# Six buffers for gathered expert rows in place of four, and padding tails written by two queues

## What is computed

```python
q, k = relu(x @ Wq.T + bq), relu(x @ Wk.T + bk)          # 16 heads of 16
v = x @ Wv.T + bv
q_, k_ = concat(q*sin, q*cos), concat(k*sin, k*cos)      # by position
kv = einsum('nld,nlm->ndm', k_, v)
z = 1 / max(einsum('nld,nd->nl', q_, k_.sum(1)), 1e-4)
x = layernorm(x + (einsum('nld,ndm->nlm', q_, kv) * z) @ Wo.T + bo)
topv, topi = top_k(x @ router_w.T, 2);  w = softmax(topv)
out = sum over the 2 chosen experts e of  w_e * (gelu(x @ w1[e].T) @ w2[e].T)   # 256 -> 512 -> 256
x = layernorm(x + out)
```

## Time and profile before

| | |
|---|---|
| median of 3 runs | 925.64 us (923.71 to 933.85) |
| the profiled execution | 932.11 us |
| its span in the trace | 930.3 us |
| PE matmuls busy | 801.9 us, 86% |
| PE weight loads busy | 761.2 us, 82% |
| DVE busy | 622.1 us, 67% |
| ACT busy | 529.6 us, 57% |
| POOL busy | 454.9 us, 49% |
| DMA moved | 108.70 MB, 117 GB/s on average |
| granted TensorE clock, mean | 0.958 of full speed |

### The profile page before, as it was taken

One profiled execution on the slowest core, in us unless ns is written; L12 is line 12 of the kernel. 1 busy time (PEld: TensorE's weight loads), 2 busy tenths in 40 slices (PEclk: granted clock), 3 DMA queues, 4 the chain that ended last, 5 costly groups with the idle time before them and its releaser, 6 DMA issues.

```text
span 930.3 us, 21892 instructions
## 1 busy us (share of the span) xinstructions
PE 801.9 (86%) x7136; PEld 761.2 (82%) x7136; DVE 622.1 (67%) x1836; ACT 529.6 (57%) x1064; POOL 454.9 (49%) x517
## 2 busy tenths in 40 slices
PE   5999999999998688888889888878999978888880
PEld 5888988988998688878888888878999978888870
DVE  3335888888888587766777566645555667767763
ACT  4556676766766445555554454444655546656653
POOL 3651566666775265554654455432343334434442
PEclk9999999999999799999999999989999999989995
DMA  6461322332332222322222232522222535546544
GB/s 193 151 220 67 104 101 93 123 108 92 113 112 76 81 86 81 97 76 92 92 74 88 75 104 75 164 78 64 81 81 81 187 132 177 202 140 215 185 175 135
DMA packets 46821, 108.70 MB, mean 117 GB/s; under 512 B 8571, under 2 KB 18815, under 8 KB 44672
## 3 DMA queue, kind: packets, MB, share of 16 engines
q1 hardware_dynamic: 31184, 65.18, 22.8%
q0 software_dynamic: 12960, 33.84, 9.9%
q10 hardware_dynamic: 2576, 8.39, 2.3%
HBM read 64.91 MB, written 46.44 MB: 120 GB/s over the span
## 4 chain that ended last, share of the span: by engine, by line
DMA 14%; PE 14%; issue 14%; DVE 6%; POOL 4%; SPq 3%; ACT 1%; POOLq 0%; DVEq 0%; ACTq 0%
PE PS L726 9%; DMA token_rows<-xg 8%; DMA xg<-expert_rows 6%; PE PS L713 3%; POOL token_rows L1710 2%; PE PS L698 2%; DVE xg L1448 2%; SPq L436 2%; DVE hT L1439 1%; DVE xgT L1431 1%; SPq L437 1%; DMA z<-token_rows 1%; POOL zve L1716 1%; POOL expert_rows L1646 1%; DVE z L1465 1%
## 5 line engine op out<-in xcount | busy, mean ns | idle before, releaser
L1710 POOL DMA_INDIRECT token_rows<-xg x142 | 165.1, 1163 | 302.4 <-DVE xg L1448 276.3
L726 PE MATMUL PS<-w,hT 128*128 x1704 | 240.3, 300 | 6.9 <-issue 5.4
L726 PEld LDWEIGHTS PS<-w,hT 128*128 128x128 f32 x1704 | 226.8, 204 | 14.0 <-issue 13.3
L713 PE MATMUL PS<-xgT,w1s 128*128 128x256 f32 x1704 | 220.6, 286 | 1.8 <-DVE xgT L1431 1.8
L713 PEld LDWEIGHTS PS<-xgT,w1s 128*128 128x128 f32 x1704 | 212.6, 194 | 2.6 <-DVE xgT L1431 2.4
L971 ACT ACTIVATE hg<-PS 128x512 f32<-128x512 f32 x142 | 84.3, 595 | 154.0 <-PE PS L713 146.5
L1646 POOL DMA_INDIRECT expert_rows<-rows,idx x128 | 135.9, 1062 | 56.2 <-issue 44.1
L1431 DVE TENSOR_TENSOR xgT<-PS,xgT 128x512 fp32r<-128x512 f32 x71 | 49.0, 691 | 139.8 <-ACT xgT L965 116.4
L1423 DVE TENSOR_TENSOR w1s<-w,w1s 128x1024 fp32r<-128x1024 f32 x71 | 86.9, 1224 | 22.2 <-issue 16.1
L698 PE MATMUL PS<-cst,xg 128*128 128x128 f32 x284 | 47.3, 292 | 57.5 <-DMA xg<-expert_rows 57.4
L1439 DVE TENSOR_TENSOR hT<-hg,hT 128x512 fp32r<-128x512 f32 x142 | 91.2, 684 | 1.7 <-issue 1.7
(11 more groups left out here) (175 smaller groups left out, 1315.5 us busy)
## 6 DMA issues: line engine op xcount, KB each, us to landing
xg<-expert_rows SPq DMA_DIRECT2D x71, 260.0 KB
z<-token_rows SPq DMA_DIRECT2D x15, 1024.0 KB
xraw<-in_xT SPq DMA_DIRECT2D x32, 256.0 KB
xtok<-in_x SPq DMA_DIRECT2D x32, 256.0 KB
out_y<-z ACTq DMA_DIRECT2D x15, 512.0 KB, 3.3
w_raw<-in_w2T SPq DMA_DIRECT2D x8, 512.0 KB, 3.9
w<-in_w1T SPq DMA_DIRECT2D x8, 512.0 KB, 5.3
token_rows<-xg POOLq DMA_INDIRECT x142
```

The source lines that it names most:

```text
L713: mm = nc.tensor.matmul(PS[:, gH[part], f * TILE:(f + 1) * TILE], w1s[:, s % 2, b, k * F + c0:k * F + c0 + P], xgT[:, s % 2, a, k, :], sta ...
L726: return nc.tensor.matmul(PS[:, gY, h * D:(h + 1) * D], hT[:, s % 2, a, k, h * P:(h + 1) * P], w2[:, bass.ds(e, 1), b, k * D:(k + 1) * D] ...
L1710: nc.gpsimd.indirect_dma_start(yd, bass.IndirectOffsetOnAxis(ap=row[:, C_DST:C_GATE].bitcast(U32), axis=0), row[:, 0:D], None, bounds_chec ...
```

## The change

`NXG` goes from 4 to 6 and the slots get a new order. `gather` reads the row number first and waits for its slot after that. The waits on the first stage, which belong to places in memory, move from steps 2 and 3 to steps 3 and 4. The eight padding tails are shared: SP writes four of them at the place where it wrote eight, ACT's queue the other four, two in each of the half steps 60 and 61 (step 30). The amount of arithmetic is the same on each engine. The places of the token loads and of the `load`s on SP's queue are counted from NXG, so a load that stood behind the gather of step s + 4 stands behind that of s + 6.

```diff
-        NXG = 4
-        XG_SLOTS = (2, 3, 1, 0)
+        NXG = 6
+        XG_SLOTS = (0, 5, 4, 3, 1, 2)
...
+        def region_tail(eng, engine, e):
+
+            row = nc.values_load(tails_i[0:1, e:e + 1], engines=[engine], min_val=0, max_val=E * REGION - TILE)
+            eng.dma_start(ex[bass.ds(row, TILE), :].rearrange("(p h) c -> p (h c)", h=2),
+                          ex[E * REGION:, :].rearrange("(p h) c -> p (h c)", h=2)).then_inc(s_tail, 16)
...
             def gather(s):
+
                 row = nc.values_load(steps[1:2, s:s + 1], engines=[ENG.SP], min_val=0, max_val=E * REGION)
+                if s >= NXG:
+                    sp.wait_ge(s_y[s % NXG], s // NXG * 32)
                 sp.dma_start(xg[:, XG_SLOTS[s % NXG]], ex[bass.ds(row, TILE), :].rearrange("(p h) c -> p h c", h=2))\
                     .then_inc(s_xg[s % NXG], 16)
-
-            def freed(s):
-
-                sp.wait_ge(s_y[s % NXG], s // NXG * 32)
...
-                if s >= NXG:
-                    freed(s)
-                if s == 2:
+                if s == 3:
                     sp.wait_ge(s_tail, 16)
                     sp.wait_ge(state_step, STATE * (B - 1) + STATE_READ)
-                if s == 3:
+                if s == 4:
                     sp.wait_ge(state_step, STATE * B)
                 gather(s)
...
             sp.wait_ge(table_step, TAILS)
-            for e in range(E):
-                row = nc.values_load(tails_i[0:1, e:e + 1], engines=[ENG.SP], min_val=0, max_val=E * REGION - TILE)
-                sp.dma_start(ex[bass.ds(row, TILE), :].rearrange("(p h) c -> p (h c)", h=2),
-                             ex[E * REGION:, :].rearrange("(p h) c -> p (h c)", h=2)).then_inc(s_tail, 16)
+            for e in range(E // 2):
+                region_tail(sp, ENG.SP, e)
...
             for s in range(FULL_STEPS, STEPS):
-                freed(s)
                 gather(s)
...
+                elif 5 <= n < 7:
+                    act.wait_ge(table_step, TAILS)
+                    for e in range(E // 2 + 2 * (n - 5), E // 2 + 2 * (n - 5) + 2):
+                        region_tail(act, ENG.Activation, e)
```

## The result

The kernel before took 924.67 us (median of 4 runs beside the changed one), the changed kernel 844.01 us (841.35 to 846.08, 4 runs). The ratio is 0.916, with a 95% interval from 0.908 to 0.924: 8.4% faster. The forecast was 863 us with 850 as its low end, so the direction and the mechanism held, and the gain was forecast 19 us too small.

A forecast was written before the change was run, and what follows sets the result against it. The four-slot gather ring was taken to hold PE, with slots waiting for sends to land. Gains of 25 + 9.5 + 2 + 29 = 65.5 us from 932.1 gave 866.6; half the 6 us offset made 863 us, range 850 to 886.

The forecast's parts named there:

- Six slots, 600 to 657: Second stage around the padding tails, 7 steps: at the clean 6.69 us a step a gain of 10.3, taken as 9.5.
- 657 to 731: Second stage, 11 steps running alone: from 6.69 towards 6.47 us a step, at most 2.4 us, taken as 2.
- 731 to 892: Second stage, 20 steps beside the last layernorm: a gain of 29 us, ends 18 and 32.
- 331 to 600: Second stage, 29 steps beside attention pairs: 23.0 us waits plus 7.1 clock, less 5 returned as other waits; gain 25.
- The offset: Profiled execution before lay 0.7% above the runs' median; up to 6 us come off, half taken.
- Reading ahead: SP's gather, row number read ahead of the slot wait: hidden, 0; 0.7 us per binding turn if slack were gone.
- Tails: Padding tails on two queues: PE's 3.9 us wait at step 33 goes; price on ACT 0 to 5.3 us, taken 1.
- Rival 1: DVE sets the pace beside the last layernorm: gain there 17 to 18, about 880 us with returned waits; chance 0.14 (shared).
- Rivals 2 to 4: The second: landings stretch beside the last layernorm, ring stays tight, 882 to 890 us, chance 0.08; others listed below.
- rival 3: No change: the gather waits for SP's order of loads, not for its slot; about 925 us, chance 0.05.
- rival 4: Slower: SP's gathers run two further ahead and their reads collide with the sends; say 940 us, chance 0.03.
- Signs: Second stage: L698 wait under 5 us, clock 0.99 or more, L726 about 0.132 us each, steps beside layernorm 6.4 to 6.7.

## Why the prediction was right in kind and too small

**The bound.** Right. The turn of the four slots held PE. The gather's wait, 51.2 us in the four stretches, is gone with six slots, and most of it is back with six slots held as four.

**Six slots, 600 to 657.** I gave 9.5 and it was 13.75. The step that failed is "7 steps at the clean 6.69". The stretch 657 to 731 looked clean since L698 waits for only 0.9 us in it, but its ring was tight. Six of its steps began with rows that had only just landed. A pair of such steps (start 664.25 to 677.59) took 13.34 us, two of after take 12.38, and the row names a wait of 0.19. So each late landing cost some 0.9 us, of which 0.16 was listed on average (0.98 / 6, by the gaps ahead of the transposes).

**657 to 731.** I gave 2, at most 2.4, and it was 5.5. Here the floor failed: "towards 6.47", which was PE's busy time over eleven. PE's busy time held the slowed matmuls behind each late landing (transposes 0.66 in place of 0.60, L726 3.23 in place of 3.11). The same 573 instructions were busy for 71.18 us before and 68.05 after. The shortest step there was 6.29; that a step with its rows in time takes 6.19 is shown by the runs with five and six slots. The same row had a better floor: PEld was busy for 68.73 us, 6.25 a step.

**731 to 892.** I gave 29 with 32 as the upper end, and it was 35.3. It is the same floor: 20 steps at 6.47 are 129.4 us, and the stretch took 125.81. With 6.19 for 6.47 the upper end would have been 20 x (8.05 - 6.19) = 37.

**331 to 600.** I gave 25 and it was 30.8. What PE was idle (length less busy time) fell from 37.4 to 18.6 us. That is 18.7 back, where I had 23.0 of gather waits less 5 of others, so this term was right in its sum. The others did return: L585 went from 1.2 to 8.4 us, L681 from 1.2 to 3.7, L562 from 6.8 to 3.6. What PE was busy fell from 231.6 to 219.5 us, 12.1 back, and this is the term that failed: I had put 7.1, from the rows of L726 alone. They gave 98.90 - 90.89 = 8.0. The rest lies in other matmuls, 1.5 us in L562 and 1.0 in the transposes of L698, against 1.3 more in L713, with the slow one of step 31; what is left can't be given to a line, since the records of the lines overlap.

**PE's busy time as a whole.** By the same subtraction the four stretches gave back 18.7 + 8.4 + 2.4 + 22.8 = 52.4 us of idle time and 12.1 + 5.3 + 3.1 + 12.5 = 33.0 of busy time. Priced were 51.2 less 5 = 46.2 us of waits and 15.6 of slowed matmuls. The other price that the prediction gives, 24 us from the clock column, would have put the forecast at 855, still 11 too high. L726 gave 227.7 - 209.3 = 18.4.

**The offset.** I took half of the 6 us between the profiled execution and the median of before. The profiled execution of after lies 0.6 us above its median: nearly all of it vanished.

**Summed up:** 866.6 was worked out for the profiled execution and 844.6 came. The four stretches missed by 5.8 + 4.25 + 3.5 + 6.3 = 19.9 us, and 2.1 lie outside them. The last three of these are the plain step of 6.19 us, for which I had 6.47 to 6.69, and the first is the price of the slowed matmuls. It is one error: I took PE's busy time under the tight ring, but for the rows of L726, as the time that the work itself needs.

**Reading ahead: 0.** Right with six slots (0.9 us between three kernels), and so was the condition beside it, that it is worth something when the slack is gone; its size then was 19 us with four slots.

**Tails.** Right in its steps: SP's four took 5.18 us (5.3), and PE didn't wait for step 33. But the split wasn't what brought that, as six slots alone brought it too. The price on ACT did not show in the time: step 31 took 11.95 and 11.93 us in the two traces with ACT's tails, and 11.95 and 11.92 in the two of the second chip with six slots and all eight on SP. ACT itself stood 4.61 us around them, most of it while its queue issued three of its tails (558.87 to 562.23). The row puts that wait down to DVE's table.

**Rival 1, DVE.** It did not take over beside the last layernorm: PE is busy 124.81 of 125.81 us there, though DVE is busy 112.97, 90%. Beside the pairs DVE did hold PE, by the order of its work and ACT's.

**Rivals 2 to 4.** Landings did stretch in the last stretch, with its 225 GB/s, but by far less than the slack. Here are the issues of the changed kernel there, with the median us to landing at the end of the row; over its whole trace they are 2.7 and 2.9:

```profile
xg<-expert_rows SPq DMA_DIRECT2D x18, 260.0 KB, 3.0
token_rows<-xg POOLq DMA_INDIRECT x40, 3.7
```

Against rival 3 the ring's turn had been the wait, and against rival 4 nothing got slower.

**Signs.** L726 at 0.130, the wait of L698 gone and the clock at 1.00 from step 32 were as said. "A step of 6.4 to 6.7 us" was not, and L585 and L562 together reached 12.0 where I had said some 10.

## What to carry to other kernels

Measure the floor of a step where its input has lain ready for a whole step. Where data arrives just in time, the listed wait is a small part of its cost (here 0.16 of about 0.9 us), and the engine's busy time is inflated too, so neither busy time nor the steps with small waits are a floor. Here the busy time of the weight loads (6.25 us a step) came nearer to the true 6.19 than that of the matmuls (6.47).

A ring is long enough when the distance in steps times the *new*, shorter step exceeds the turn. Past that point another slot buys next to nothing (5 to 6 slots: some 4 us), and each saving within the turn, worth 2% while the ring bound, buys nothing that the runs can tell. When the ring has let go, look at once at what order the next engine does its work in: another 1.5% lay there for a few moved lines.

## What the runs showed of the hardware that I had not expected

- Where PE stopped for even 0.2 us for a gather, its matmuls started again slowly at full granted clock; what delays them the trace doesn't say. From the transposes to the next matmuls pass 0.86 us in place of 0.36, with 0.2 of it listed as "issue", and the 24 matmuls behind take 3.23 in place of 3.11 us. The timeline of before, with the next, undisturbed step under it:

```profile
670.78 0.66 PE L698 MATMUL PS<-cst,xg 128*128 128x128 f32 x4 [0.19 <-DMA xg<-expert_rows]
671.64 3.23 PE L726 MATMUL PS<-w,hT 128*128 x24 [0.20 <-issue]
...
677.59 0.60 PE L698 MATMUL PS<-cst,xg 128*128 128x128 f32 x4
677.95 3.11 PE L726 MATMUL PS<-w,hT 128*128 x24
```

- The same program took 3.2 to 3.3% longer on one chip than on another with six slots (843.65 and 870.82 us, 842.77 and 870.54). Steps alone took the same 6.19 us on both. The kernel before took 1.7 to 2.3% longer there. So a kernel whose waits are gone can show a chip's differences more than one that waits anyway.
